# Relative keys made earlier in an attention and mixture-of-experts kernel: a fourth quad at the start, and the first four quads of each one-tile row

## The chip, the cores and the metric

The kernel runs on 1 core of one Trainium2 chip. The metric is the device time of one execution in microseconds; lower is better. The kernel before takes 776.27 us (median of 3 runs, 775.61 to 785.23). All times inside the kernel come from one profiled execution, which took 775.52 us.

## The reference, cut to what matters

x has 8 batches of 512 tokens with 128 channels; there are 16 heads of 8 dimensions. The distance between two tokens is cut off at zero on one side, and the table of relative keys has 128 rows, so that distances of 127 and more share the last row.

```python
qkv = layernorm(x) @ w_attn                     # q, k, v: (B, H, T, d)
rel = jnp.tril(idx[:, None] - idx[None, :])     # an index past the table takes its last row
rk = embk[rel]; rv = embv[rel]
att = einsum('bhtd,bhsd->bhts', q, k) * scale + einsum('bhtd,tsd->bhts', q, rk)
att = softmax(where(causal, att, -inf))
y = einsum('bhts,bhsd->bhtd', att, v) + einsum('bhts,tsd->bhtd', att, rv)
x = x + y.transpose(...) @ w_proj
x = x + experts(layernorm(x))                   # 8 experts, the best 2 of each token, and 2 shared
```

## The kernel before, in words

**Setup.** `qkv_part` makes queries, keys and values in four groups of two batches. Queries and keys are cut into three bfloat16 parts each and written to the DRAM tensor `qk_rows`, values to `v_dram`. From there `load_first(b, n)` reads queries (n = 0) or keys (n = 1) of batch b into `qb` or `kb`, in three transfers of 0.39, 0.20 and 0.20 MB (one of 48 partitions, two of 24).

**Attention.** The work is cut into quads: four heads of one batch and one tile row of 128 queries. There are 128 quads, 8 for each tile row and group; the tile rows come in the order 2, 0, 1, 3 (`ROWS`), so quads 0 to 7 are in row 2 (three tiles of keys), 8 to 15 in row 0 (one tile; these are the one-tile rows), 16 to 23 in row 1, 24 to 31 in row 3. The next group begins with quad 32, and so on; quads 40, 72 and 104 open the other one-tile rows. A quad is cut into units: 4 units of one head in rows 2 and 3, 2 units in row 1, and 1 unit of four heads in row 0. There are 352 units (`UNITS`); `FIRST[q]` is the first of quad q. Each engine walks through steps m = 0, 1, 2, ..., with one unit in each. In step m VectorE adds the relative scores to the scores of unit m and takes the minimum (L1071), ScalarE takes the exponentials (L994), TensorE makes the scores of unit m + 1 (`qk`, L833) and turns the probabilities of unit m - 3 (`tp`, L845). Two engines copy them (L983, L1056), and `av` (L862) multiplies by the values.

**The relative keys of a quad** go a long way before VectorE can add them: TensorE multiplies its queries by the key table (`rel`, L820) into a PSUM bank, ScalarE copies the product into one of five buffers `relS` (`rel_copy`, L970), a DMA writes it with a skewed pitch into one of eight slots of the DRAM tensor `w_slots` (`put_rel`, L687, 0.26 MB), and a second DMA reads it back into one of five buffers `near` (`get_near`, L695, 0.52 MB, in row 0 half of that). `scores_min` waits for this read (`near_in`). Such a read can be issued only when VectorE is done with the quad five before.

**What sets the order.** `rel_slots` gives the earliest step of each quad's `rel`: 8 steps ahead of its first unit in rows 0 and 1, 14 steps in rows 2 and 3. `schedule` then puts the side operations into steps (at most one `rel` in a step, apart from step 0) and gives them three PSUM banks by turns (`BANK`); `BEFORE` names the use of the bank that must have been read first, and `take` waits for it. The quads of step 0 are made during setup: quads 0, 1 and 2, with a copy on ScalarE between (L970 x3), and TensorE waits for these copies in the middle of its last turn of x (`first_copied`). `REL_AT` is the step of a quad's `rel`, and `READ_AT` that of its read: 3 steps later in rows 0 and 1, 5 in rows 2 and 3.

**The DMA queue.** SyncE issues every transfer of this kernel on one queue, in program order, and waits in it: a `put_rel` for its copy on ScalarE, a `get_near` for the write into its slot. In one step SP does its reads, then its writes, then a piece of setup work that was put off (`PIECES_AT`: rows of queries and keys of later groups, 0.26 MB each, or values, 0.59 MB). `load_v` reads 0.59 MB.

TensorE's `rel` of quads 4 to 7 waits for all queries of batch two (`q_first[1]`); the scores of quad 4 wait for its keys.

Of the kernel before, what the change touches and what calls it, by code (L numbers as in the profile page):

```python
# [26 lines left out]
QUADS = NH // 4  # L27
Q_PART = [0, 0, 1, 1, 2, 0]
K_PART = [0, 1, 0, 1, 0, 2]
NPART = len(Q_PART)  # L30
# [12 lines left out]
NEAR = 5  # L43
RSLOTS = 5
# [4 lines left out]
MISC = 3  # L49
# [8 lines left out]
FIRST = [UNITS.index((q, 0)) for q in range(NQ)] + [NU]  # L58


def row(q):

    return ROWS[q // QUADS % NI]


def last(q):

    return FIRST[q + 1] - 1
# [10 lines left out]
def rel_slots():  # L79

    at = []
    for q in range(NQ):
        ahead = 8 if row(q) <= 1 else 14
        reload = last(q - QUADS) + 4 if q // QUADS % NI == 0 and q >= QUADS else 0
        at.append(max(reload, FIRST[q] - ahead, 1 if q >= MISC else 0, *at[-1:]))
    return at


REL_SLOT = rel_slots()

RVN = 8
# [14 lines left out]
def schedule():  # L106
# [16 lines left out]
    for m in range(SLOTS):  # L123
        for item in [d for d in due if d[0] <= m]:
# [33 lines left out]
OPS, BANK, BEFORE, LAST = schedule()  # L158
SLOT_OF = {op: m for m in range(SLOTS) for op in OPS[m]}
REL_AT = [SLOT_OF["rel", q] for q in range(NQ)]  # L160
READ_AT = [max(REL_AT[q] + (3 if row(q) <= 1 else 5), FIRST[max(q - NEAR + 1, 0)]) if REL_AT[q] else 0
           for q in range(NQ)]


# [381 lines left out]
def attention_part(nc, t, x, w_attn, w_proj, e_k, e_k127, e_k127h, e_v, e_v127, part_of_row, qk_rows, v_dram, w_slots,  # L546
                   x1_dram, experts_of):
    with ExitStack() as ctx:
# [18 lines left out]
        first = qkv_part(nc, t, ctx, x, w_attn, w_proj, e_k, e_k127, e_k127h, e_v, e_v127, part_of_row, qk_rows, v_dram,  # L567
                         w_slots)
# [79 lines left out]
        with nc.Block() as block:  # L648

            @block.sync  # L650
            def _(sp):
# [10 lines left out]
                def load_first(b, n):  # L662
                    src = qk_rows[b, n, :, :, :].rearrange("r (d s u j) t -> s (r d) u (j t)", s=2, u=H // 4, j=2)
                    for side in range(2):
                        for at, first_row, rows in PLACES[side]:
                            if n == 0:
                                dst = qb[at:at + rows, b * H:(b + 1) * H, :].rearrange(
                                    "p (u s j) t -> p u s (j t)", s=2, j=2)[:, :, side, :]
                            else:
                                dst = kb[at:at + rows, b * H // 2:(b + 1) * H // 2, :].rearrange(  # L670
                                    "p (u j) t -> p u (j t)", j=2)
                            sp.dma_start(dst, src[side, first_row:first_row + rows]).then_inc((q_first, k_first)[n][b], 16)
# [6 lines left out]
                def put_rel(q):  # L679
                    k = q % WSLOTS  # L680
                    sp.wait_ge(rel_done, q + 1)
                    if q >= WSLOTS:
                        sp.wait_ge(near_in[(q - WSLOTS) % NEAR], 16 * ((q - WSLOTS) // NEAR + 1))
                    whole = w_slots[k]
                    pitch = 4 * P * 2
                    dst = bass.AP(whole.tensor, whole.offset + 2, [[pitch + 2, P], [2 * P * 2, 2], [1, 2 * P]])
                    sp.dma_start(dst, relS[:, q % RSLOTS, :, :, :].rearrange("p a j h -> p a (j h)")).then_inc(w_out[k], 16)  # L687

                def get_near(q):
                    k = q % WSLOTS  # L690
                    c = P if row(q) == 0 else 0
                    sp.wait_ge(w_out[k], 16 * (q // WSLOTS + 1))
                    if q >= NEAR:
                        sp.wait_ge(min_done, HEADS_BEFORE[FIRST[q - NEAR + 1]])
                    sp.dma_start(near[:, q % NEAR, :, 2 * P + c:4 * P, :].rearrange("p a c h -> p a (c h)"),  # L695
                                 w_slots[k][:, :, c:2 * P, :].rearrange("p a c h -> p a (c h)")
                                 ).then_inc(near_in[q % NEAR], 16)
# [32 lines left out]
                now = REL_AT.count(0)  # L730
                for q in range(now):
                    put_rel(q)
                first["values"](sp, 1)
                load_first(1, 0)
                first["row"](sp, 1, 1, NPART - 1)
                for q in range(now):
                    get_near(q)
                load_first(1, 1)
                sp.wait_ge(*first["masks_out"](2))
# [1 line left out]
                for m in range(SLOTS):  # L741
                    for q in range(NQ):
                        if READ_AT[q] == m > 0:
                            get_near(q)
# [788 lines left out]
```

## Time and profile before

| | us |
|---|---|
| median of 3 runs | 776.27 |
| profiled execution, whole | 775.52 |
| its span, from the first to the last instruction | 773.8 |
| VectorE (DVE) busy | 587.7 (76%) |
| TensorE (PE) busy, modelled ends | 698.8 (90%) |
| ScalarE (ACT) busy | 515.4 (67%) |
| mean granted TensorE clock | 0.979 |

Attention runs to about 540 us, then the experts follow. The DMA line gives the mean busy share of 16 DMA engines in tenths for each fortieth of the span (19.3 us). Idle time of an engine is put down to what came last: "<-DMA near<-w_slots" is a wait for the read of relative keys.

### The profile page before, as it was taken

What the parts mean: (1) busy time and instruction counts of PE and PEld (TensorE: products, weight loads), DVE (VectorE), ACT (ScalarE), POOL (GpSimd) and SP (SyncE); (2) the same over time, 40 slices, a digit from 0 to 9 for tenths busy, and PEclk for the clock granted to TensorE, in tenths of its full rate; (3) what the DMA queues carried; (4) which work ended last, traced back from release to release, by engine and by line L of the source; (5) the groups of instructions that cost most, each with busy time, mean ns of one, the idle gap of its engine ahead of it and who ended that gap; (6) DMA issues with size and microseconds to landing.
All of it is one profiled execution on the core that took longest, in us unless ns stands there. A gap on an engine that the chain in (4) does not pass through costs nothing. (4 is left out here: it accounts for less than half of the span.)

```text
span 773.8 us, 27143 instructions
## 1 busy us (share of the span) xinstructions
PE 698.8 (90%) x10368; PEld 507.2 (66%) x10368; DVE 587.7 (76%) x2036; ACT 515.4 (67%) x1032; POOL 255.6 (33%) x253
## 2 busy tenths in 40 slices
PE   4767787999889999988998988998999999999997
PEld 3445565777666677766776766776666666666665
DVE  7956586888778788887888878888567776676676
ACT  3676777888788788897887898887325343443331
POOL 9443354434346434445543545523000000000000
PEclk9878999999999999999999999999999999999999
DMA  9999899789899788788878778851000000000000
GB/s 260 269 277 335 289 306 316 225 230 283 271 282 297 246 236 256 219 253 245 234 227 255 214 227 271 248 174 56 3 22 28 28 0 28 28 15 0 14 15 14
DMA packets 118864, 139.27 MB, mean 180 GB/s; under 512 B 8977, under 2 KB 87313, under 8 KB 118545
## 3 DMA queue, kind: packets, MB, share of 16 engines
q1 hardware_dynamic: 118736, 137.54, 58.6%
q8 instruction: 84, 1.38, 0.7%
q14 instruction: 44, 0.35, 0.1%
HBM read 82.26 MB, written 55.25 MB: 178 GB/s over the span
## 5 line engine op out<-in xcount | busy, mean ns | idle before, releaser
L1071 DVE CUSTOM_DVE_ANT_0 ps<-ps,near 128x128 f32<-128x128 f32 (+3 forms) x512 | 245.2, 510 | 96.1 <-PE ps L833 66.5
L994 ACT ACTIVATE work<-ps,nmin 128x128 f32<-128x128 f32 (+3 forms) x512 | 249.2, 543 | 61.9 <-DVE nmin L1071 54.3
L845 PE MATMUL ps<-ident,work 128*128 128x128 f32 x1280 | 202.9, 278 | 13.9 <-issue 11.6
L845 PEld LDWEIGHTS ps<-ident,work 128*128 128x128 f32 x1280 | 157.8, 143 | 36.6 <-issue 17.0
L791 POOL TENSOR_SCALAR_AFFINE_SELECT work<-work 128x512 f32<-128x512 f32 x96 | 61.2, 638 | 242.2 <-ACT work L983 207.8
L833 PE MATMUL ps<-kb,qb 128*128 128x128 bf16 (+3 forms) x512 | 131.4, 309 | 9.8 <-ACT work L994 9.2
L1388 ACT ACTIVATE near<-ps 128x512 f32<-128x512 f32 x80 | 47.5, 595 | 133.8 <-PE ps L1353 133.7
L795 POOL TENSOR_TENSOR work<-work 128x512 f32<-128x512 f32 x96 | 124.2, 1294 | 8.0
L1056 DVE COPY work<-ps 128x512 f32<-128x512 f32 (+1 forms) x192 | 123.4, 643 | 1.2 <-PE ps L845 0.9
L1363 PEld LDWEIGHTS ps<-work,near 128*128 128x128 f32 x640 | 82.6, 192 | 34.3 <-issue 31.7
L983 ACT ACTIVATE work<-ps 128x512 f32<-128x512 f32 (+1 forms) x160 | 90.0, 563 | 16.0 <-PE ps L845 15.4
L862 PE MATMUL ps<-work,vb 128*9 128x128 f32 x2560 | 96.6, 278 | 2.4 <-ACT relS L970 1.6
L1408 DVE TENSOR_TENSOR near<-near,ps 128x512 f32<-128x512 f32 x80 | 54.9, 687 | 50.7 <-ACT near L1388 36.4
L970 ACT ACTIVATE relS<-ps 128x512 f32<-128x512 f32 x128 | 84.5, 661 | 11.5 <-PE ps L820 7.7
L1363 PE MATMUL ps<-work,near 128*128 128x128 f32 x640 | 83.1, 275 | 0.0
L1353 PE MATMUL ps<-near,work 128*128 128x512 f32 x160 | 82.8, 599 | 0.0
L1354 PE MATMUL ps<-near,work 128*128 128x512 f32 x160 | 81.7, 592 | 0.0
L1423 DVE SCALAR_TENSOR_TENSOR near<-ps,near 128x128 f32<-128x128 f32 x256 | 71.9, 343 | 5.3
L862 PEld LDWEIGHTS ps<-work,vb 128*9 128x9 f32 x2560 | 58.0, 91 | 25.0 <-issue 20.5
L1071 DVE DVE_READ_ACCUMULATOR2_ANT nmin<- 128x1 f32 x512 | 72.5, 142 | 0.0
L878 PE MATMUL ps<-tv,work 128*32 128x8 f32 x4096 | 58.5, 179 | 13.7 <-issue 13.7
L878 PEld LDWEIGHTS ps<-tv,work 128*32 128x32 f32 x4096 | 47.4, 111 | 31.8 <-issue 28.5
(111 smaller groups left out, 624.4 us busy)
## 6 DMA issues: line engine op xcount, KB each, us to landing
near<-w_slots SPq DMA_DIRECT2D x96, 512.0 KB, 5.4
w_slots<-relS SPq DMA_DIRECT2D x128, 256.0 KB, 4.6
qk_rows<-work SPq DMA_DIRECT2D x36, 256.0 KB, 5.1
near<-w_slots SPq DMA_DIRECT2D x32, 256.0 KB, 4.6
qk_rows<-y SPq DMA_DIRECT2D x9, 256.0 KB, 6.1
qb<-qk_rows SPq DMA_DIRECT2D x24, 96.0 KB
kb<-qk_rows SPq DMA_DIRECT2D x24, 96.0 KB
qb<-qk_rows SPq DMA_DIRECT2D x48, 48.0 KB
```

Of the source, the lines that this page charges most:

```text
L795: nc.gpsimd.tensor_tensor(dst, ptmp[:, :, :], pT[:, q % 2, :, i * P:(i + 1) * P], ALU.add).then_inc(pc_done, 1)
L833: ins = nc.tensor.matmul(qk_ps[:, m % 3, h * wide:(h + 1) * wide], qb[:, n, i * P:(i + 1) * P], kb[:, n // 4 * 2 + n % 2, 0:wide], start=T ...
L845: ins = nc.tensor.transpose(tp_ps[:, m % 2, n * P:(n + 1) * P], prob[:, m % PROBS, n * P:(n + 1) * P], ident[:, :])
L862: ins = nc.tensor.matmul(bank[32 * h:32 * h + VD, a * P:(a + 1) * P], vb[:, g % 2, b * NI + j, n * VD:(n + 1) * VD], pT[:, q % 2, h, j * P ...
L878: ins = nc.tensor.matmul(bank[32 * tq:32 * tq + NH, a * D:(a + 1) * D], pcT[:, e % 2, tau, :], tv[:, tau, :], start=True, stop=True)
L970: nc.scalar.activation(relS[:, q % RSLOTS, :, :, :].rearrange("p a j h -> p a h j"), misc("rel", q).rearrange("p (a h j) -> p a h j", a=2, ...
L983: nc.scalar.activation(pT[:, q % 2, n * w:n * (w + 1), 0:wide], tp_ps[:, m % 2, 0:n * wide].rearrange("p (h s) -> p h s", h=n), ACT.Copy). ...
L994: ins = nc.scalar.activation(prob[:, m % PROBS, h * wide:(h + 1) * wide], qk_ps[:, m % 3, h * wide:(h + 1) * wide], ACT.Exp, bias=nmin[:, ...
L1056: nc.vector.tensor_copy(pT[:, q % 2, n * w:n * (w + 1), 0:wide], tp_ps[:, m % 2, 0:n * wide].rearrange("p (h s) -> p h s", h=n)).then_inc( ...
L1071: nc.vector.tensor_tensor_reduce(out=scores, in0=scores, in1=near[:, q % NEAR, a, 4 * P - wide:4 * P, r], scale=1.0, scalar=3e38, op0=ALU. ...
L1353: nc.tensor.matmul(h1_ps[k % 2], w1_sb[:, m, :], rhs, start=True, stop=True).then_inc(h1_ready, 1)
L1363: ins = nc.tensor.matmul(y_ps[k % 2][:, n * P:(n + 1) * P], hT[:, (NM * c + m) % 4, n * P:(n + 1) * P], w2_sb[:, m, :], start=(m == ms[0]) ...
```

## The change

```diff
@@ rel_slots
         ahead = 8 if row(q) <= 1 else 14
+        if row(q) == 0 and q % QUADS < 4:
+            ahead = 14 - q % QUADS
         reload = last(q - QUADS) + 4 if q // QUADS % NI == 0 and q >= QUADS else 0
-        at.append(max(reload, FIRST[q] - ahead, 1 if q >= MISC else 0, *at[-1:]))
+        at.append(max(reload, FIRST[q] - ahead, 1 if q >= RSLOTS - 1 else 0, *at[-1:]))
@@ READ_AT
-READ_AT = [max(REL_AT[q] + (3 if row(q) <= 1 else 5), FIRST[max(q - NEAR + 1, 0)]) if REL_AT[q] else 0
+READ_AT = [max(REL_AT[q] + (3 if row(q) == 1 or row(q) == 0 and q % QUADS >= 4 else 5), FIRST[max(q - NEAR + 1, 0)]) if REL_AT[q] else 0
            for q in range(NQ)]
@@ the sync program
                 first["values"](sp, 1)
+                first["row"](sp, 1, 1, NPART - 1)
+                get_near(0)
+                get_near(1)
                 load_first(1, 0)
-                first["row"](sp, 1, 1, NPART - 1)
-                for q in range(now):
+                for q in range(2, now):
                     get_near(q)
                 load_first(1, 1)
```

Three things move. Quad 3's `rel` goes from step 1 to step 0, into the setup, so `now` is 4 and not 3. The queries of batch two are loaded behind the reads of quads 0 and 1. In every one-tile row the first four quads have their `rel` in steps 18, 20, 22, 24 and not 24, 25, 26, 27 (first group; 106 to 112 in place of 112 to 115 in the second, and so on), and their reads in steps 23, 25, 27, 29 in place of 27, 28, 29, 30. Their first units are 32 to 35. Since the banks are given out by turns, many uses of a bank get another one.

The first place is SP's queue at the end of setup, before the change. L687 is `put_rel`, L317 values, L672 `load_first` (qb queries, kb keys), L312 a row piece, L695 `get_near`.

```order
L687 DMA w_slots<-relS 128x2x256 x3
L317 DMA v_dram<-work 128x1152
L672 DMA qb<-qk_rows 48x4x1024
L672 DMA qb<-qk_rows 24x4x1024 x2
L312 DMA qk_rows<-relS 128x2x512
L695 DMA near<-w_slots 128x2x512 x3
L672 DMA kb<-qk_rows 48x4096
L672 DMA kb<-qk_rows 24x4096 x2
L687 DMA w_slots<-relS 128x2x256
```

The same place after the change; every line number is higher by 2.

```order
L689 DMA w_slots<-relS 128x2x256 x4
L319 DMA v_dram<-work 128x1152
L314 DMA qk_rows<-relS 128x2x512
L697 DMA near<-w_slots 128x2x512 x2
L674 DMA qb<-qk_rows 48x4x1024
L674 DMA qb<-qk_rows 24x4x1024 x2
L697 DMA near<-w_slots 128x2x512 x2
L674 DMA kb<-qk_rows 48x4096
L674 DMA kb<-qk_rows 24x4096 x2
```

The fourth write stands with the first three, the fourth read (which stood some way behind, in step 6) ahead of the keys, and the queries behind two reads.

The second place is SP's queue around steps 14 to 28, before the change: from the write of quad 7 over the reads of quads 6 and 7 to the first read of a one-tile row (128x2x256).

```order
L687 DMA w_slots<-relS 128x2x256
L695 DMA near<-w_slots 128x2x512 x2
L317 DMA v_dram<-work 128x1152 x2
L312 DMA qk_rows<-work 128x2x512
L687 DMA w_slots<-relS 128x2x256 x2
L312 DMA qk_rows<-work 128x2x512
L687 DMA w_slots<-relS 128x2x256
L695 DMA near<-w_slots 128x2x256
```

And after the change, from the same write to the same read.

```order
L689 DMA w_slots<-relS 128x2x256
L697 DMA near<-w_slots 128x2x512
L689 DMA w_slots<-relS 128x2x256
L697 DMA near<-w_slots 128x2x512
L319 DMA v_dram<-work 128x1152
L689 DMA w_slots<-relS 128x2x256
L319 DMA v_dram<-work 128x1152
L689 DMA w_slots<-relS 128x2x256
L697 DMA near<-w_slots 128x2x256
```

Quad 8's write now stands ahead of quad 7's read, quads 9 and 10's between the values, and the first read of the one-tile row comes ahead of two row pieces.

The third place is TensorE at the end of setup. Before (L820 is `rel`, L368 the last turn of x, L387 values, L377 and L381 queries and keys, L833 scores):

```order
L820 MATMUL ps<-te,qb 128x128 x12
L368 MATMUL ps<-ident,work 128x128 x8
L387 MATMUL ps<-vb,work 128x128 x8
L377 MATMUL ps<-work,vb 128x512 x2
L381 MATMUL ps<-work,vb 128x512 x2
L387 MATMUL ps<-vb,work 128x128 x8
L833 MATMUL ps<-kb,qb 128x384 x2
L820 MATMUL ps<-te,qb 128x128 x4
```

After:

```order
L824 MATMUL ps<-te,qb 128x128 x16
L370 MATMUL ps<-ident,work 128x128 x8
L389 MATMUL ps<-vb,work 128x128 x8
L379 MATMUL ps<-work,vb 128x512 x2
L383 MATMUL ps<-work,vb 128x512 x2
L389 MATMUL ps<-vb,work 128x128 x8
L837 MATMUL ps<-kb,qb 128x384 x3
L824 MATMUL ps<-te,qb 128x128 x4
```

Four matrix products move from behind the first scores to the front. Quads 2 and 3 both take the bank that the quad before them in this bank has to leave (bank 5: quads 0, 2 and 3, one behind the other's copy). The last row is now quad 4's `rel`, which waits for the queries of batch two.

## Rows read from the trace of the kernel before

**Rows 1.** The page, part 2: DMA busy tenths and GB/s in 40 slices.

```profile
DMA  9999899789899788788878778851000000000000
GB/s 260 269 277 335 289 306 316 225 230 283 271 282 297 246 236 256 219 253 245 234 227 255 214 227 271 248 174 56 3 22 28 28 0 28 28 15 0 14 15 14
```

**Rows 2.** Waits of DVE, whole span: us in total, times, longest.

```profile
DVE ps L1071 <- PE ps L833: 66.5, 102, 2.2
...
DVE ps L1071 <- DMA near<-w_slots: 27.5, 18, 4.5
```

**Rows 3.** Timeline of DVE, 50 to 110 us: start, us, what, idle before.

```profile
53.73 0.57 DVE L1071 CUSTOM_DVE_ANT_0 ps<-ps,near 128x384 f32<-128x384 f32 x1 [3.45 <-DMA near<-w_slots]
...
55.56 0.57 DVE L1071 CUSTOM_DVE_ANT_0 ps<-ps,near 128x384 f32<-128x384 f32 x1 [0.18 <-PE ps L833]
...
68.02 0.57 DVE L1071 CUSTOM_DVE_ANT_0 ps<-ps,near 128x384 f32<-128x384 f32 x1 [4.48 <-DMA near<-w_slots]
...
84.22 0.57 DVE L1071 CUSTOM_DVE_ANT_0 ps<-ps,near 128x384 f32<-128x384 f32 x1 [0.91 <-DMA near<-w_slots]
...
92.40 0.30 DVE L1071 CUSTOM_DVE_ANT_0 ps<-ps,near 128x128 f32<-128x128 f32 x1 [4.46 <-DMA near<-w_slots]
...
95.83 0.30 DVE L1071 CUSTOM_DVE_ANT_0 ps<-ps,near 128x128 f32<-128x128 f32 x1 [2.32 <-DMA near<-w_slots]
...
99.49 0.30 DVE L1071 CUSTOM_DVE_ANT_0 ps<-ps,near 128x128 f32<-128x128 f32 x1 [1.13 <-DMA near<-w_slots]
...
102.68 0.30 DVE L1071 CUSTOM_DVE_ANT_0 ps<-ps,near 128x128 f32<-128x128 f32 x1 [1.54 <-DMA near<-w_slots]
...
109.32 0.43 DVE L1071 CUSTOM_DVE_ANT_0 ps<-ps,near 128x256 f32<-128x256 f32 x1 [0.22 <-issue]
```

**Rows 4.** Timeline of DVE, first and last such wait of the later one-tile rows.

```profile
224.74 0.30 DVE L1071 CUSTOM_DVE_ANT_0 ps<-ps,near 128x128 f32<-128x128 f32 x1 [0.62 <-DMA near<-w_slots]
...
465.09 0.30 DVE L1071 CUSTOM_DVE_ANT_0 ps<-ps,near 128x128 f32<-128x128 f32 x1 [0.70 <-DMA near<-w_slots]
```

**Rows 5.** Timeline of ACT: the three copies of relative keys in setup.

```profile
36.52 1.82 ACT L970 ACTIVATE relS<-ps 128x512 f32<-128x512 f32 x3
```

**Rows 6.** Timeline of PE: last product of setup, and quad 4's.

```profile
37.29 0.38 PE L820 MATMUL ps<-te,qb 128*128 128x128 bf16 x4 [1.92 <-ACT relS L970]
...
51.69 0.61 PE L820 MATMUL ps<-te,qb 128*128 128x128 bf16 x4 [0.76 <-DMA qb<-qk_rows]
```

**Rows 7.** Timeline of SP's queue: queries, reads, quad 3's write and read, quad 8's read.

```profile
41.63 2.19 SPq L672 DMA_DIRECT2D qb<-qk_rows  x3
...
44.30 2.83 SPq L695 DMA_DIRECT2D near<-w_slots  x3
...
55.58 0.38 SPq L687 DMA_DIRECT2D w_slots<-relS  x1
...
62.70 0.54 SPq L695 DMA_DIRECT2D near<-w_slots  x1
...
88.84 0.53 SPq L695 DMA_DIRECT2D near<-w_slots  x1
```

**Rows 8.** Windows: us, busy of PE, PEld, DVE, ACT, POOL, PEclk, DMA share, GB/s.

```profile
44.00:48.00 4.00, 3.69 (x22) 2.44 (x20) 1.37 (x2) 3.33 (x4) 3.01 (x2) 1.00 1.01 233
...
56.00:60.00 4.00, 4.00 (x29) 3.23 (x32) 3.69 (x13) 3.95 (x9) 0.63 (x1) 0.72 0.98 230
...
72.00:76.00 4.00, 4.00 (x36) 2.98 (x24) 2.42 (x8) 2.06 (x5) 0.75 (x2) 0.59 1.07 369
...
88.00:92.00 4.00, 2.42 (x27) 1.79 (x31) 0.00 (x0) 3.10 (x7) 1.49 (x2) 0.62 0.61 205
...
96.00:100.00 4.00, 2.41 (x28) 1.66 (x32) 2.87 (x22) 2.98 (x10) 1.30 (x2) 0.90 1.05 339
```

**Rows 9.** The page, part 6: KB each, median us to landing.

```profile
near<-w_slots SPq DMA_DIRECT2D x96, 512.0 KB, 5.4
w_slots<-relS SPq DMA_DIRECT2D x128, 256.0 KB, 4.6
```

## The prediction

> **What bounds the kernel now.** I read the table of DVE's waits first, since DVE does the step that needs the relative keys. Over the span it waited 66.5 us for scores from PE and 27.5 us, in 18 waits, for the read of relative keys [rows 2]. The change is aimed at the second sum, so I looked in DVE's timeline for where it lies. Most of it falls before 103 us: 3.45 us ahead of the first unit of all, 4.48 us at quad 3 (unit 12, at 68.02 us), 0.91 us at quad 7, and then, in the one-tile row, 4.46, 2.32, 1.13 and 1.54 us at quads 8, 9, 11 and 12 [rows 3]. The four of the one-tile row make 9.45 us. In the three later one-tile rows there are seven such waits of 0.17 to 1.33 us, the first at 224.74, the last at 465.09 us, 4.77 us in all [rows 4]. So 22.2 us of waits stand where the change could reach them (3.45 + 4.48 + 9.45 + 4.77).
>
> A wait for a DMA can have two reasons: the transfer was issued late, or the DMA engines were full. The page shows them 80 to 90% busy or more until 500 us [rows 1], and the windows of 4 us tell both reasons apart. In 72 to 76 us they moved 369 GB/s at a share of 1.07, in 96 to 100 us 339 at 1.05: full. In 88 to 92 us they moved 205 at 0.61, in which DVE did nothing: late issue. In 56 to 60 us the share is 0.98 but the rate only 230 [rows 8]. So early issue helps as far as there are such gaps to fill; past that, DVE waits for bytes, and the order of the same bytes matters little.
>
> **Part 1, quad 3 made in setup.** Copies take 1.82 / 3 = 0.61 us, and the three end at 36.52 + 1.82 = 38.34 us [rows 5]. The fourth product goes to the bank of the third and so waits for its copy: it starts at 38.34, takes 0.38 us [rows 6], and PE goes on with the turn of x at 38.7 where it did at 37.5. ACT's fourth copy ends at 39.4. I charge 1.2 us to the end of setup: DVE is free at 53.73 - 3.45 = 50.28 us now [rows 3], and then at 51.5. It is hidden as long as the first read lands later than that.
>
> **Part 2, queries behind two reads.** SP issued the queries at 41.63 and the first read at 44.30 us [rows 7], and quad 4's product found the queries at 51.69 [rows 6], DVE the read at 53.73. Between these two stand a row piece and the read, 0.79 MB in 2.04 us, some 385 GB/s, so transfers on the full engines land about in the order of issue. Now the first read has 0.79 MB of queries less ahead of it, at the 233 GB/s of that stretch [rows 8] 3.4 us, and one more write of 0.26 MB, at 350 GB/s 0.7 us. It lands at 53.73 - 3.4 + 0.7 = 51.0, and DVE starts at 51.5, 2.2 us sooner. But the queries now have the write (0.26), a row piece (0.26) and two reads (1.05) ahead, 1.57 MB, 4.4 us: they land at 51.6 + 4.4 = 56.0. Quad 4's `rel` stands ahead of the scores of unit 3 on PE, so these come behind it at about 56.5, and DVE has unit 3 at 57.0 instead of 55.56 [rows 3]. Behind the same wait stand, on ACT, the copy of quad 4 and the exponentials of unit 2, and on SP quad 4's write, which holds every row piece behind it. The 2.2 us are lost again and 1.4 more.
>
> **Part 3, no wait at quad 3.** Its write went out at 55.58, and SP stood until 62.70 before it could issue the read [rows 7]. Now both go out before 50 us, and the 4.48 us go. DVE is then 4.48 - 1.4 = 3.1 us early at unit 12. From there the bytes take over: up to quad 4's read the same 0.26 and 0.52 MB pieces are ahead of it in both kernels, and it gets sooner only by what the engines do in their poor stretch, which the keys and reads queued by then fill: 4 us at 350 in place of 230 GB/s are 0.48 MB or 1.4 us, and I add 0.6 for the 4 us behind. So quads 4 to 7 have their keys 2 us sooner, quad 7 at 82.2 instead of 84.22 us.
>
> **Part 4, the one-tile row.** Now a write takes 4.6 us and a read 5.4 [rows 9], and quad 8 has 8 steps of some 0.9 us between product and use, too few; with 14 to 11 steps that chain fits. Past that it is bytes. From quad 7's read to quad 12's stand the values (2 x 0.59 MB) and 17 transfers of 0.26: 5.6 MB. At 345 GB/s, between the two full windows, that is 16.3 us: quad 12 at 98.5 against 102.68, 4.2 us sooner. Up to quad 16's read it is 7.7 MB, 22.4 us, to 104.6; quad 16's first unit stood at 109.32 [rows 3], some 5 us later. What fills the way is the empty stretch in 88 to 92 us: SP stood there for quad 8's write until 88.84 [rows 7]. I take 5 us at the end of the first one-tile row. The ends: if the engines give only the 306 GB/s of the slice behind 97 us [rows 1], the 7.7 MB take 25.2 us and quad 16 is 1.9 us sooner; if bytes never bind, all of 4.48 + 9.45 - 1.4 = 12.5.
>
> PE and ACT do the same work as before in these steps, only spread (every second step has a `rel`, not four in a row), so I cost it at nothing. The writes of quads 8, 9 and 10 stand ahead of quad 7's read and the values: quad 7's read waits behind a copy due in step 18 while it is itself used in step 28, so the wait is covered, and 0.26 MB costs 0.7 us, which is within part 3.
>
> **Part 5, the later one-tile rows.** 4.77 us of waits. Behind each the next thing late is PE's scores, DVE's largest wait in any case [rows 2], so I take 3 us of them; 0.5 to 4.77 are the ends. Other banks: three uses (`av` in steps 142, 230 and 318) now come one step behind a copy of relative keys; at most a copy's 0.6 us each, taken as nothing beside 14 places of the same distance that go.
>
> **The sum**, against the profiled execution: 775.52 - 5 - 3 = 767.5 us. That execution was 0.75 us under the median of the runs, so a median would come at 768.3; I say 768.
>
> The Trainium skill, page "DMA: Bandwidth & Descriptors", section Specifications, gives two ceilings: 435 GB/s for the fabric and about 358 for a core's share of HBM. By the first, part 4's 7.7 MB would take 17.7 us and the gain there would be 9.7 us, by the second 21.5 and 5.9. Rows 8 show 369 at most, a little over the second and far from the first; my sum uses neither.
>
> **Rivals.**
> All waits go. If the engines had room wherever they were asked early, the sum is 4.48 + 9.45 + 4.77 - 1.4 = 17.3 us, 758 us. For it: 88 to 92 us, and PE's clock of 0.59 in 72 to 76 us [rows 8], behind the idle time at quad 3, would be whole again. Against it: a share of 1.05 in the very stretch. The ceiling of 435 GB/s above points this way.
> The gain is swallowed. The queries land 2 us later still, the first row piece and quad 4's write go later with them, and the bytes behind leave 1 us of part 4 and 1.5 of part 5: 773 us. For it: PE, ACT and SP all stand behind one wait, and the 24-partition loads are slow (233 GB/s). Against it: the queue would be filled meanwhile.
> Slower. The place is PE's wait for the queries of batch two ahead of unit 3; each us that they land past 56 is a us on everything, since SP issues nothing behind quad 4's write. From 64 us on it eats all 8 us; landing at 66.5 gives 778. Against it: values, two writes, a row piece, two reads and the queries are 3.2 MB; from 44.3 us on, at 233 GB/s throughout, they are through by 58.
> That the change does not do what it says, that is, that the reads are issued earlier but don't land earlier, is the second rival.
>
> **How the numbers follow.** Forecast (gain 5 to 11, 764.5 to 770.5) 0.58; swallowed (771 to 776) 0.27; all waits go 0.07; slower 0.08. The range for 8 in 10 runs from 762 to 776: it takes in most of the swallowed case and the lower part of what lies between forecast and full gain. 2% is 15.5 us, about what a measurement of this kernel can tell from no change: faster by that (below 760.7) only in most of the full gain, 0.05; slower 0.02; within 0.93.
>
> **What would show it.** Right: DVE's first unit at 51 to 52 us with little wait, unit 3 at 57 behind a wait of PE for qb<-qk_rows of some 3 us, no wait of DVE at quad 3, smaller waits for near at quads 4 to 6, DVE at quad 8 by 87 to 88 us, rates near 350 GB/s without a gap in 76 to 104, some wait left at quads 11 to 16, and under 2 us of waits in the later one-tile rows. Wrong: unit 3 before 55 or after 59; quad 16 before 101 or after 108; or DVE as early as forecast at 110 us and the end not, which would mean that PE's scores give it back.

## The result: 0.7% faster

The changed kernel takes 775.36 us in the median of 20 runs (771.54 to 784.36), beside 782.05 us for the kernel before in 20 runs of its own. The ratio is 0.9929, with a 95% interval of 0.9908 to 0.9949: some 5.5 us of gain, real and small. All ratios here leave out runs more than 1.5% above the fastest of the same kernel, so this one is not quite that of the two medians, and one run left out of e17 took 1658.36 us, for which nothing here shows a cause. Two later comparisons of the same pair gave 0.9947 (0.9913 to 0.9981) and 0.9970 (0.9941 to 0.9999). The forecast, 768 against 776.27, is a ratio of 0.989. The direction was right; the gain came out at about two thirds of the forecast or less, and, as the experiments show, largely from other places than the prediction said.

One thing has to be known before two profiles are held side by side. The three runs shown of the kernel before (median 776.27) lay low: with more runs its median is 779 to 782, and its profiled execution of 775.52 us is among its quickest. The profiled execution of the changed kernel took 775.50 us. Both spans are 773.8 us, so single traces can't show the gain; they show only what each start looks like, and I read later parts from several profiles.

### The profile page after: what moved, and what is told of

It is laid out like the page before. It is cut to its first block and busy times, and to the rows that moved or that the text cites. A ratio compares the mean times of both kernels' runs of the same rounds, so it can differ in the third digit from the quotient of the medians.

```text
span 773.8 us, 27144 instructions
## 1 busy us (share of the span) xinstructions
PE 699.8 (90%) x10368; PEld 508.3 (66%) x10368; DVE 589.5 (76%) x2036; ACT 515.4 (67%) x1032; POOL 255.9 (33%) x253
## 5 line engine op out<-in xcount | busy, mean ns | idle before, releaser
L1075 DVE CUSTOM_DVE_ANT_0 ps<-ps,near 128x128 f32<-128x128 f32 (+3 forms) x512 | 245.2, 510 | 90.7 <-PE ps L837 71.4
L987 ACT ACTIVATE work<-ps 128x512 f32<-128x512 f32 (+1 forms) x160 | 90.5, 566 | 16.3 <-PE ps L849 15.5
L1075 DVE DVE_READ_ACCUMULATOR2_ANT nmin<- 128x1 f32 x512 | 72.1, 141 | 0.0
```

What stands on the lines that cost most here:

```text
L987: nc.scalar.activation(pT[:, q % 2, n * w:n * (w + 1), 0:wide], tp_ps[:, m % 2, 0:n * wide].rearrange("p (h s) -> p h s", h=n), ACT.Copy). ...
L1075: nc.vector.tensor_tensor_reduce(out=scores, in0=scores, in1=near[:, q % NEAR, a, 4 * P - wide:4 * P, r], scale=1.0, scalar=3e38, op0=ALU. ...
```

## The profile after

Waits of DVE over the whole span, the two rows that answer to [rows 2]:

```profile
DVE ps L1075 <- PE ps L837: 71.4, 100, 5.0
...
DVE ps L1075 <- DMA near<-w_slots: 17.2, 18, 3.0
```

Waits for relative keys fell from 27.5 to 17.2 us, waits for scores rose from 66.5 to 71.4, the longest from 2.2 to 5.0. DVE's timeline, for [rows 3]:

```profile
52.77 0.56 DVE L1075 CUSTOM_DVE_ANT_0 ps<-ps,near 128x384 f32<-128x384 f32 x1
...
59.45 0.57 DVE L1075 CUSTOM_DVE_ANT_0 ps<-ps,near 128x384 f32<-128x384 f32 x1 [5.03 <-PE ps L837]
...
72.86 0.57 DVE L1075 CUSTOM_DVE_ANT_0 ps<-ps,near 128x384 f32<-128x384 f32 x1 [1.05 <-DMA near<-w_slots]
...
78.31 0.57 DVE L1075 CUSTOM_DVE_ANT_0 ps<-ps,near 128x384 f32<-128x384 f32 x1 [2.44 <-DMA near<-w_slots]
...
91.23 0.30 DVE L1075 CUSTOM_DVE_ANT_0 ps<-ps,near 128x128 f32<-128x128 f32 x1 [0.56 <-DMA near<-w_slots]
...
102.49 0.30 DVE L1075 CUSTOM_DVE_ANT_0 ps<-ps,near 128x128 f32<-128x128 f32 x1 [2.96 <-DMA near<-w_slots]
...
111.63 0.43 DVE L1075 CUSTOM_DVE_ANT_0 ps<-ps,near 128x256 f32<-128x256 f32 x1 [1.94 <-PE ps L837]
```

These are units 0, 3, 16, 20, 32, 36 and 40. The first unit no longer waits, unit 3 waits 5 us, the wait at unit 12 is gone, new ones stand at units 16 and 20 (quads 4 and 5), the 4.46 us at unit 32 are 0.56, and quad 12 (unit 36) now has the longest wait for a read, 2.96 us. PE, for [rows 6], and SP's queue, for [rows 7]:

```profile
39.76 0.38 PE L824 MATMUL ps<-te,qb 128*128 128x128 bf16 x4 [0.81 <-ACT relS L974]
...
58.48 0.61 PE L824 MATMUL ps<-te,qb 128*128 128x128 bf16 x4 [5.21 <-DMA qb<-qk_rows]
```

```profile
45.30 1.60 SPq L697 DMA_DIRECT2D near<-w_slots  x2
46.95 1.47 SPq L674 DMA_DIRECT2D qb<-qk_rows  x3
48.46 1.18 SPq L697 DMA_DIRECT2D near<-w_slots  x2
...
59.79 0.38 SPq L689 DMA_DIRECT2D w_slots<-relS  x1
```

The queries go out from 46.95 on and have landed at 58.48, some 10 us behind the last issue. Until then PE stands in front of quad 4's product, and SP in front of its write, which goes out at 59.79. The windows, for [rows 8], show what the DMA engines did and what the wait did to PE's clock (columns as there):

```profile
52.00:56.00 4.00, 0.32 (x1) 0.10 (x1) 2.42 (x8) 1.84 (x3) 3.73 (x2) 0.76 1.08 185
56.00:60.00 4.00, 1.51 (x9) 1.37 (x10) 0.55 (x2) 0.87 (x2) 0.00 (x0) 0.50 1.08 274
60.00:64.00 4.00, 4.00 (x21) 3.45 (x20) 3.16 (x11) 3.27 (x8) 0.47 (x1) 0.50 0.96 229
...
88.00:92.00 4.00, 3.95 (x59) 3.14 (x58) 3.26 (x15) 3.98 (x9) 1.70 (x3) 1.00 1.07 362
```

The gap of 88 to 92 us is filled (362 GB/s for 205), as forecast. The stretch in which the queries move shows 185 GB/s at a full share, and after PE's idle time its granted clock stays at the lower level, 1.2 GHz, until 64 us.

The forecast also said that no gap would be left between 76 and 104 us, and there one stands: the engines moved 226 GB/s in 80 to 84 us, where the kernel before moved 314 (135 and 260 in two further profiles of the changed kernel, e16 and e18 below). SP's queue shows what it stood for:

```profile
80.00:84.00 4.00, 3.45 (x36) 2.15 (x37) 2.05 (x7) 3.18 (x8) 1.92 (x2) 0.68 0.80 226
```

```profile
74.29 0.49 SPq L689 DMA_DIRECT2D w_slots<-relS  x1
...
81.33 0.53 SPq L697 DMA_DIRECT2D near<-w_slots  x1
```

These are the write and the read of quad 7. The write landed at 81.32 us, 7.0 us behind its issue. The read waits for that, and so does all that SP has to issue behind it. In the kernel before it was quad 8's write that SP waited for in this way, until 88.84 [rows 7].

## The experiments

Each ran with the kernel before on the same chip. "Part A" is quad 3 in setup, "part B" the queries behind two reads, "part C" the one-tile rows. Unit starts are those of a unit's first custom instruction in DVE's timeline (L1071 or L1075).

**One part at a time: e1, e2, e3, e4.** e1 is part C alone, e2 part A alone, e4 part B alone, e3 the changed kernel without part B:

```diff
@@ e3_no_queries against the changed kernel (e1: also q >= MISC again; e2: also without the `ahead` and READ_AT edits)
+                load_first(1, 0)
                 first["row"](sp, 1, 1, NPART - 1)
-                get_near(0)
-                get_near(1)
-                load_first(1, 0)
-                for q in range(2, now):
+                for q in range(now):
                     get_near(q)
```

> Only the relative keys of the one-tile rows are made 14 to 11 steps ahead; quad 3 and the queries stay as before. Theory A (the queries of batch two come late in the changed kernel and take back what quad 3 gives): the one-tile part alone is worth nearly all of the measured gain, ratio to before 0.993, and DVE's wait at quad 3 (4.5 us) stands, waits at quads 8 to 11 shrink from 7.9 us to under 4. Theory B (up to quad 12 the bytes on the DMA engines set the time, whatever the order): the same ratio, 0.993 to 0.996, but unit 36 (quad 12) starts at 102 to 103 us as in both kernels. Theory C (the gain of the change lies in the start): ratio 0.998 or above.

> Only quad 3 is made with the first three; queries of batch two ahead of all four reads, one-tile rows as before. Theory A: PE's wait for the queries is under 2 us, unit 3 starts by 57 us, no wait at quad 3 (unit 12), unit 12 by 66 us; some 2 us of that are left at unit 32, ratio 0.997. Theory B: unit 12 is as early, but DVE waits for near at quads 4 to 8 instead and unit 32 is where it was (92 us), ratio 1.000. The setup ends 1.2 us later in both.

> The changed kernel with the queries of batch two put back ahead of the reads (quad 3 in setup and one-tile rows as changed). Theory A: unit 3 at 56 to 57 us and not 59.5, all later units until 40 some 2 to 3 us earlier than in the changed kernel, ratio to before 0.989 to 0.990. Theory B: units 3 to 12 earlier by 2 to 3 us, but DVE then waits longer for near at quads 4 to 6, unit 36 at 102 us, ratio 0.993 as the changed kernel.

> Only the queries of batch two are put behind the first two reads; three quads in setup, one-tile rows as before. Theory A: PE waits some 4 to 5 us for the queries ahead of unit 3, unit 3 at 58 to 59 us, everything behind it 2 to 3 us later than before, ratio 1.003. Theory B: ratio 1.000, the first units start 2 us earlier, unit 12 at 68 us and unit 32 at 92 us as before.

Measured: e1 0.9864 (0.9814 to 0.9914), e2 0.9995 (0.9960 to 1.0030), e3 0.9888 (0.9843 to 0.9933), e4 1.0034 (0.9997 to 1.0071). So, as far as these intervals tell, the gain is all part C's; part A alone shows none, as the theory has it by which the transfers, and not quad 3's place, set when quads 4 and 5 are there, and part B is on the losing side, though its interval touches 1. Part A is the instructive one. In e2 unit 12 starts at 64.0 us, 4 us sooner than before, and then:

```profile
69.18 0.57 DVE L1071 CUSTOM_DVE_ANT_0 ps<-ps,near 128x384 f32<-128x384 f32 x1 [1.74 <-DMA near<-w_slots]
...
74.78 0.57 DVE L1071 CUSTOM_DVE_ANT_0 ps<-ps,near 128x384 f32<-128x384 f32 x1 [2.59 <-DMA near<-w_slots]
```

That is DVE's timeline of e2 at units 16 and 20. The wait at quad 3 has come back as waits at quads 4 and 5, and unit 32 is at 92.2 us, as before. In e4 PE waited 6.26 us for the queries, unit 3 started at 58.5 us.

**Is it PE's row that makes the queries dear? e9.** The changed kernel, with quad 4's product three steps later.

```diff
-1 if q >= RSLOTS - 1 else 0, *at[-1:]
+5 if q == RSLOTS - 1 else 0, *at[-1:]
```

> The changed kernel, but quad 4's relative keys go from step 2 to step 5 (its first unit is 16), so that PE reaches the scores of units 3 to 5 without the queries of batch two. If the late queries cost time only because quad 4's product stands in PE's row ahead of unit 3, PE's wait of 5.2 us for qb<-qk_rows moves behind unit 5 and shrinks to under 3 us, unit 3 starts at 55 to 56 us and not 59.5, ratio to before 0.989 against 0.993. If bytes bind all the same, unit 16 is at 72 to 73 us as in the changed kernel and the ratio stays 0.993.

Measured: 0.9943 (0.9909 to 0.9978), the changed kernel's own value. PE has no wait for the queries left, unit 3 starts at 53.99 us, 5.5 us sooner, unit 12 at 62.4, and all of it is lost at once, as DVE's timeline of e9 shows at unit 16:

```profile
72.43 0.57 DVE L1075 CUSTOM_DVE_ANT_0 ps<-ps,near 128x384 f32<-128x384 f32 x1 [6.59 <-DMA near<-w_slots]
```

Unit 16 is where it was (72.86). Quad 4's write went out at 57.51 us, 2.3 us sooner than in the changed kernel (59.79), but it landed at 66.77 (67.47 there), so that it took 9.3 us in place of 7.7; the read went out at 66.79 and landed at 72.30. The same time for unit 16 from starts that differ by 5 us says that DVE's early start has no value until quad 4's keys can be there. Further on, e9 is ahead of the mean of the three profiles of the changed kernel, by 1.8 us at unit 28 and 3.2 at unit 40, and 1.1 us behind it at unit 56. That is one profile.

**Which one-tile rows pay? e5, e6.** Part C for quads 8 to 11 alone, and for the later three rows alone (the condition gets `q // QUADS == 1`, or `q // QUADS > 1`).

> Quads 8 to 11 alone are made 14 to 11 steps ahead; the three later one-tile rows, quad 3 and the queries stay as before. Theory A (the split of the prediction): this row is worth 3 to 5 us, ratio to before 0.994 to 0.996. Theory B (bytes bind up to quad 16, and what the first row gives is given back by unit 136): ratio 0.998 to 1.000, and the later rows carry the gain.

> Quads 40 to 43, 72 to 75 and 104 to 107 alone are made 14 to 11 steps ahead, the first one-tile row as before. Theory A: the three rows together are worth 3 us, ratio 0.996. Theory B: they carry most of the 8 to 10 us that the one-tile part gave, ratio 0.987 to 0.990.

Measured: e5 0.9989 (0.9949 to 1.0028), e6 0.9959 (0.9924 to 0.9994). The later rows pay; for the first no gain is shown, though the two intervals overlap. The two together say 0.995 and part C as a whole 0.986 to 0.991; the intervals leave room for that, but it is no clean sum. The traces say it better than the totals. Over thirteen profiles with part C in the later rows and five without (both kernels and the experiments; e11 and e13, with their other order, not among them), the same stretches took, in us:

```
units        with part C there      without             difference
112 to 128   22.6 (21.9 to 23.3)    25.0 (24.5 to 25.5)   2.4
200 to 216   24.0 (23.0 to 25.6)    25.4 (24.4 to 26.8)   1.5
288 to 304   22.7 (22.1 to 23.5)    25.5 (24.6 to 26.5)   2.8
```

That is 6.7 us from the three mean differences. Nearly half of it, 3.2 us, lies in the first eight units of each, ahead of the one-tile row (112 to 120: 9.5 with, 10.5 without; 200 to 208: 9.5 and 10.7; 288 to 296: 9.5 and 10.5): there four products and four copies of relative keys no longer stand in four steps one behind the other, and DVE's waits for scores fell to 0.81 us in each from 1.85 to 2.01. The rest is DVE's waits for reads in the one-tile rows themselves, 3.6 us in the three rows together where it was 6.5; they shrank, but did not go. Some of the gain is given back in the eight units just ahead, into which the products moved: 104 to 112, 192 to 200 and 280 to 288 take 0.1, 0.5 and 0.5 us more. From 104 to 128, 192 to 216 and 280 to 304 together it is 96.0 us (93.8 to 97.4) with part C and 101.6 (99.8 to 102.8) without: 5.6 us, and the two ranges do not touch. It stays until the end: from unit 104 to the last unit it is 337.1 us against 343.2.

**What holds quad 12? e7, e10, e11, e13, e14.** All have part C alone and one thing more. e7 loads the values of group 1 in step 61 and not 11; e10 also sends the six row pieces of group 2 in steps 37 to 47 and not 23 to 33; e14 the same in steps 33 to 43; e11 is e10 with quad 12 made 10 steps ahead, e13 is part C with just that.

```diff
@@ e7, and in e10, e11, e14
-                        if m == last(q) + 8 and ...
+                        if m == last(q) + (8 if q else 58) and ...
@@ e10, e11 (e14: 10 and not 14)
-    at.update({19 + 2 * k: [piece] ...
+    at.update({19 + 2 * k + (14 if k >= 2 else 0): [piece] ...
@@ e11, e13 (READ_AT takes the fifth quad along)
-        if row(q) == 0 and q % QUADS < 4:
+        if row(q) == 0 and q % QUADS < 5:
```

> The one-tile part alone (the kernel that had 0.986), and besides the values of group 1 (0.59 MB), used from unit 88 on, are loaded in step 61 and not in step 11, that is, behind the full stretch. If the bytes on the DMA engines set the time of quads 5 to 12, 0.59 MB at 350 GB/s are 1.7 us: units 20 to 40 come 1.5 us sooner, ratio 0.984. If the chain write, landing, read sets it, nothing changes: ratio 0.986 as without it.

> The one-tile part alone, with less to move in the full stretch: the values of group 1 are loaded in step 61, and the six row pieces of group 2 go out in steps 37 to 47 and not 23 to 33 (together 2.2 MB less ahead of quad 12, 6 us at 350 GB/s). If bytes and SP's row of issues set the time of quad 12, DVE's wait there (2.7 to 4.3 us) goes, unit 40 starts by 103 us against 106 to 109, ratio 0.983 or below, unless the steps behind 40 give it back. If quad 12's own chain (product in step 28, write, read) sets it, the wait stays at 2 us or more.

> As e10, and quad 12 too is made 10 steps ahead (step 26, not 28). If quad 12's own chain sets unit 36, its wait goes here and not in e10, and unit 40 is 2 us earlier than in e10. If bytes did, both are alike, within 1 us.

> The one-tile part alone, and the fifth quad of every one-tile row (12, 44, 76, 108) too is made 10 steps ahead and not 8. If quad 12's own chain sets unit 36, DVE's wait there falls from 2.7 to 4.3 us to under 2 and unit 40 comes 1 to 2 us sooner (105 us); ratio 0.986 to 0.988, the best so far. If bytes do, the wait stays and the ratio is 0.988 to 0.990.

> e10 mended: values of group 1 in step 61, row pieces of group 2 in steps 33 to 43, so that they have left before near_values(0) in step 46 waits for them (in e10 it waited 11.7 us). If bytes ahead of quad 12 matter, unit 40 by 104 us and ratio 0.985 or below; if not, unit 40 at 106 us and 0.988 to 0.991 as the one-tile part alone.

Measured: e7 0.9916 (0.9882 to 0.9950), unit 32 at 86.2 us and unit 40 at 105.5, sooner than the 87.7 to 90.9 and 106.1 to 109.7 of part C alone, but not in the total. e10 0.9993 (0.9951 to 1.0035) and e11 0.9975 (0.9935 to 1.0015) ran into a wait that I had overlooked. DVE's timeline of e10:

```profile
129.98 0.64 DVE L1082 STREAM_TRANSPOSE work<-ps 128x256 f32<-128x256 f32 x1 [11.73 <-DMA qk_rows<-work]
```

`near_values(0)` writes where the row pieces lie, and has to wait until the last has left. Their totals say nothing, their starts up to unit 44 do. e14, meant as the mend, gave 0.9921 (0.9886 to 0.9956) and still had 4.63 us of that wait. With the row pieces out of the way, units 32 to 36 take 9.0 (e10), 8.1 (e11) and 9.4 us (e14), against 11.1 to 11.4 in part C alone: quad 12 comes sooner without the bytes. But units 36 to 40 then take 8.3 to 9.6 us for 7.0 to 7.4, so that quads 13 to 16 are waited for instead. e11 against e10 was to tell quad 12's own chain from the bytes: the wait at unit 36 is the same (1.66 and 1.62 us), but unit 40 is 3.6 us sooner, of which 1.5 us stand already at unit 32, so the pair decides nothing. In e13, without the lighter queue, making quad 12 itself sooner does nothing (3.48 us of wait there, unit 40 at 106.3; ratio 0.9884, 0.9854 to 0.9914). SP's queue in e12, which is part C alone, shows quad 12's way:

```profile
88.19 0.42 SPq L689 DMA_DIRECT2D w_slots<-relS  x1
...
93.87 0.84 SPq L697 DMA_DIRECT2D near<-w_slots  x1
```

This is quad 12's write and, six other transfers later, its read. ScalarE's copy had ended at 83.84 us, and DVE was done with quad 7's buffer at 85.4. The write stood in SP's row until 88.19 and landed at 93.36; the read went out 0.5 us behind that, landed at 98.62, and unit 36 started at 98.76. So quad 12 has 4.4 us in SP's row, 5.2 us of write and 4.8 us of read, with half a us between the two. In e13 the copy ended 1.6 us sooner, at 82.19, and the write went out and landed sooner too (86.51 and 92.10), but the read stood in the row until 93.63 and landed at 99.16. How much of all this is bytes (362 and 344 GB/s in 88 to 92 and 96 to 100 us of the changed kernel), how much SP's issue times and how much its waits for writes to land, these runs don't separate.

**How much one execution differs from another: e8.** The kernel before, unchanged.

> The kernel before, unchanged, as if it were another: ratio 1.000 within its interval. Its profile shows how far the starts of units 12, 40, 128 and 296 differ from one execution to another of the same program; I expect 1 to 3 us, since whole runs differ by 10.

Measured: 1.0001 (0.9965 to 1.0038), runs from 773.8 to 788.9 us. In its profile DVE waited at quad 3:

```profile
67.19 0.57 DVE L1071 CUSTOM_DVE_ANT_0 ps<-ps,near 128x384 f32<-128x384 f32 x1 [2.77 <-DMA near<-w_slots]
```

2.77 us, where the first profile had 4.48 [rows 3], and 2.81 us ahead of unit 32 where that had 4.46. Unit 128 was 4.7 us later than in the first. So part of the 22.2 us of waits on which the sum was built was that one execution's.

**Side by side: e12, e15, e16, e17, e18.** e12 and e17 are e1 again, e15 is e3 again, e16 and e18 are the changed kernel.

> The one-tile part alone once more, the same kernel that gave 0.9864 from 6 runs. The sum of its halves (0.9989 and 0.9959) and the difference of the changed kernel to the one with the queries alone (0.9929 to 1.0034) both say less: I expect 0.989 to 0.991, 3 us less than the first measurement.

> The changed kernel with the queries of batch two back ahead of the reads, once more. If the late queries cost 3 us in the end, this is 0.003 to 0.005 below e16 in the ratio; if bytes even it out by quad 12, both are alike within 0.002.

> The changed kernel once more, beside e15 on the same chip: 0.993 as in its 20 runs. In the profile PE again waits 4 to 6 us for the queries, with unit 3 at 58 to 60 us and PE's clock at half speed behind that wait.

> The one-tile part alone. If quad 3 and the late queries take back some 3 us of its gain, this is 0.003 to 0.006 below e18 in the ratio, 0.988 to 0.990; if they cost nothing, both are within 0.002.

> The whole change beside e17 on one chip: 0.993 to 0.995 as in its earlier runs; 0.988 to 0.990 if it is as good as the one-tile part alone.

Measured: e12 0.9898 (0.9840 to 0.9956). On one chip e15 0.9943 (0.9908 to 0.9977) and e16 0.9947 (0.9913 to 0.9981): the late queries cost nothing that this pair can show. On another e17 0.9913 (0.9867 to 0.9958) and e18 0.9970 (0.9941 to 0.9999): by this pair parts A and B together take back some 4 us of part C, but the intervals overlap, so that it is likely and not shown. PE's waits for the queries were 5.21, 5.65 and 3.78 us in the three profiles of the changed kernel.

Means of the unit starts over the profiles of each kind (in us; none: before, e8, e6; C: e1, e5, e12, e17; A and C: e3, e15; all: the changed kernel, e16, e18) put the first 140 us in one view:

```
unit      0     3    12    16    28    32    36    40    56
none   53.9  55.7  67.5  70.5  83.9  91.9 102.1 109.0 138.1
C      53.9  55.7  67.5  70.7  83.9  88.9 100.3 107.6 136.9
A, C   54.7  56.5  64.9  70.0  83.9  88.5 100.3 107.8 136.2
all    52.1  58.5  67.0  71.5  85.8  90.1 101.5 109.5 138.4
```

Whatever the start looks like, units 16 and 28 stand within 2 us of each other. Part A's 2.6 us at unit 12 are 0.7 at unit 16 and 0.0 at unit 28. Part B makes unit 0 2.6 us sooner than A and C alone and every unit from 3 to 56 some 1.2 to 2.2 us later. Part C's 3.0 us at unit 32 are 1.4 at unit 40. The means rest on two to four profiles each, and three profiles of the changed kernel differ by 4.4 us at unit 40 (107.23 to 111.63), so a difference of 1 to 2 us there is weakly shown.

## Why the prediction was right and wrong

**The end of setup (part 1)** was right: the copies ran as three and one, with the fourth product at 39.76 us, 1.2 us behind the third. DVE was free for its first unit at 51.0 us in the mean of the thirteen profiles with three quads in setup, and at 52.2 in the seven with four, where 1.2 us had been charged. That the copies began at 37.80 us and not at 36.52 is no doing of the change: over the profiles of all kernels, the one before among them, this start lies between 36.46 and 37.80.

**The queries (part 2)** had the right mechanism and the wrong size. PE was to wait some 3 us, with the queries in at 56.0 and unit 3 at 57.0; they came at 58.5, 57.4 and 56.7 us in three profiles, and unit 3 stood at 59.5, 58.4 and 57.7. The term at fault is the working "1.57 MB, 4.4 us": I moved the queries' start by the bytes put ahead of them and kept their own duration. In the profiled execution they came some 10 us behind the last issue, where it had been 7.9 before the change, while the engines moved 185 GB/s in 52 to 56 us (242 and 206 in e16 and e18).

**Quads 4 to 7 two us sooner (part 3)** is the step that failed. I counted bytes and took the engines' poor stretch in 56 to 60 us as room that the earlier transfers would fill. They did run without a gap in 56 to 64 us, but at 274 and 229 GB/s: the slow stretch moved with the slow transfers (queries and keys, of 48 and 24 partitions) and was not room. What the sum left out is quad 4's own way: copy, write, landing, read, landing, each behind the other. In the changed kernel's profile the copy ended at 59.77 us, the write went out at 59.79 and landed at 67.47, the read went out at 67.48 and landed at 72.73, and unit 16 started at 72.86. From the end of the copy to unit 16 it is 12.3 to 13.1 us in the three profiles of the changed kernel, and 13.7 and 14.6 in the two of the kernel before. So the way became a us or two shorter, much as the count of bytes had it; but quad 3 in setup makes the copy no sooner (56.2 to 57.2 us in e2 and e3, 56.4 and 56.5 before), and the late queries of part B make it later, 58.0 to 59.8. The 4.6 and 5.4 us of [rows 9] were used for quad 8 alone, and for quads 4 and 7 the write took 7.7 and 7.0. The wait for quad 7's write is also what left the engines at 226 GB/s in 80 to 84 us. Quad 7's unit 28 came at 87.05, 85.57 and 84.80 us in the three profiles, where the prediction had 82.2. Without part B it comes at 83.9, just as before (the table): part A moves a wait from quad 3 to quads 4 and 5. The +2 us taken for parts 1 to 3 were in truth some -2 at unit 40 (107.6 against 109.5 in the table), and in the total between nothing (e15, e16, for part B) and about -4 (e17, e18, for both). If the latter is real, where the other 2 us or so arise is open; the stretches there differ between executions by as much.

**The first one-tile row (part 4)**: forecast 3 us from this part, measured 1.4 at unit 40, and -0.0011 of the ratio with an interval that holds zero (e5). Right was that quads 8 to 11 would lose their waits (unit 32 3.0 us sooner) and that something would be left at quads 11 to 16; too small was how much. 345 GB/s over 5.6 MB put quad 12 at 98.5 us from a quad 7 at 82.2, 16.3 us; in the four profiles with part C alone it is 16.4 us from unit 28 to unit 36 in the mean (15.5 to 17.6), where it was 18.2. The length was right, and the gain small because its start was not sooner than before. That bytes alone make this length is not shown: quad 12's write and read, one behind the other, fill 10 us of it. Quad 16's first unit stood at 111.63, 109.72 and 107.23 us in three profiles of the changed kernel, in two of them past the 108 us that the prediction had named as its sign of being wrong. (The two gains worked out from ceilings, 9.7 and 5.9 us, start from the rounded 5; from 82.2 and 109.32 us they would be 9.4 and 5.6. No other number used them.)

**The later one-tile rows (part 5)**: forecast 3 us, measured 5.6 over the three stretches from 104, 192 and 280 on (e6's total says 3.2, 0.5 to 5.9). I took two thirds of 4.77 us of waits for reads, and these did shrink by 2.9 us in the mean, from 6.5 to 3.6; the size was right, partly by luck, since the one execution from which the 4.77 us came had the least such waits of the five, and the changed kernel's profiles still have 2.3 to 3.6 us, where under 2 had been forecast. What failed is the term put at nothing: "PE and ACT do the same work as before in these steps, only spread, so I cost it at nothing". Spread, it is 1.0 to 1.2 us quicker in the eight units ahead of each of the three rows and 0.1 to 0.5 us slower in the eight before those, some 2 us net. With the 1.4 us of unit 40 the 5.6 make 7.0 us, a ratio of 0.991, which lies in the interval of each of the three measurements of part C alone. For the whole change unit 40 is 0.5 us later than before (109.5 against 109.0), which leaves 5.1 us, a ratio of 0.9935, in two of its three intervals.

So the sum, 5 and 3, was right in neither term. That the direction and two thirds of the size came out is in part luck: what was put at nothing made up for some of what parts 1 to 4 did not give. Of the rivals, "the gain is swallowed" was nearest for the start: the queries later still, quad 4's write behind them. Its 773 us would be a ratio of 0.996; of the three measurements, 0.9929 and 0.9947 lie between it and the forecast, and 0.9970 just beyond it. "All waits go" is refuted by the waits at units 16, 20 and 36. "Slower" was refuted as a total, though for part B alone (1.0034, 0.9997 to 1.0071) it has the sign.

A version that is faster than the kernel before, and looks faster than the whole change, came out of it: part C alone, 0.9864, 0.9898 and 0.9913 in three comparisons, against 0.9929 to 0.9970 of the whole change. Only e17 and e18 set the two side by side, and their intervals overlap.

## What to carry to other kernels

In a stretch in which a transfer queue is full, a wait that is taken away at one place returns at the next read: before counting it, ask at which later unit two versions must meet again, and compare there. Where data go through DRAM and back, add up that chain, landing times included, and ask what its first step waits for. What pays is an earlier start in places where the queue has empty windows, and where side work was bunched. And a wait read from one execution is a sample: the same program showed 4.5 and 2.8 us at the same place.

## What the runs showed of the hardware that I had not expected

- The loads to 48 and 24 partitions went with slow stretches of engines that read as fully busy: 185 GB/s at a share of 1.08 while the queries of batch two were on the way, against 344 and 362 at 1.08 and 1.07 in windows with transfers over 128 partitions. That the number of partitions is the reason, and not the layout of the rows that they read, no run separates. A busy share near 1 does not mean that bytes move at the full rate.
- With the engines full, a write of 0.26 MB took 7.7 us from issue to landing (quad 4) and 9.3 us in e9, against a median of 4.6 us [rows 9], and the read of it can go out only then.
- Behind PE's wait of 5.2 us its granted clock fell to the lower level (0.50 in 56 to 64 us), but no cost of that can be seen: units 4 to 8 took 3.9 to 4.3 us in the three profiles of the changed kernel, and 3.4 to 4.4 us in profiles of other kernels without such a wait.
- Runs of one program spread over 15 us (773.8 to 788.9) with nothing changed, nearly three times the gain that was to be measured.
